# A four-layer graph network on one core: operands of VectorE moved to PSUM, and the last pass's factors moved to ScalarE

## The reference

```python
# layer 0: attention with clipped scores, 8 heads of 16
score = exp(clip(sum(K[src] * Q[dst]) / 4, -5, 5));  out = sum_dst(V[src] * score) / (sum_dst(score) + 1e-6)
# layer 1: edge features through a small network, weights from the degrees
agg = sum_dst((x[src] + relu(edge_attr @ W1e) @ W2e) * w[src] * w[dst])
# layer 2: radial weights of each edge from two silu layers, times scalars and vectors of the source
msg = combine(w_edge, xs[src], xv[src], direction);  out = sum_dst(msg) @ W_out
# layer 3: attention by channel, with a softmax over the edges of a node
e = leaky_relu(feat_src[src] + feat_dst[dst]);  a = exp(e - max_dst(e)) / sum_dst(...);  out = sum_dst(a * v[src])
```

## Time and profile before

| | before |
|---|---|
| median of 3 runs | 5067.57 us (5067.40 to 5072.91) |
| the profiled execution | 5068.24 us, its span 5066.5 us |
| PE, DVE, ACT, POOL busy | 3567.9, 3633.2, 2770.5, 3623.2 us |

### The profile page before, as it was taken

How to read it: one execution, slowest core, us unless ns; L and a number is a source line. 1 busy time by engine, 2 the same in 40 slices (tenths; PEclk the granted TensorE clock), 3 DMA queues, 4 the chain that set the end, 5 groups by cost and what they waited for, 6 DMA issues and landing times. The chain is left out here.

```text
span 5066.5 us, 96049 instructions
## 1 busy us (share of the span) xinstructions
PE 3567.9 (70%) x20064; PEld 2948.3 (58%) x20065; DVE 3633.2 (72%) x8844; ACT 2770.5 (55%) x6960; POOL 3623.2 (72%) x3861
## 2 busy tenths in 40 slices
PE   5444444453376666666778888888879999999993
PEld 4444444443265555555556666666657777777772
DVE  5666666666654444444677777777759999999998
ACT  2444444444632222222467666666648888888885
POOL 3777777775677777777367777777727877777773
PEclk7777777776687777777879999999889999999996
DMA  6444444443333333333121121122137777777772
GB/s 184 156 154 155 154 153 150 152 154 99 114 87 77 79 78 78 78 78 79 33 63 56 56 56 56 56 56 57 52 98 194 194 195 196 195 196 196 196 195 56
DMA packets 491118, 596.80 MB, mean 118 GB/s; under 512 B 127483, under 2 KB 349165, under 8 KB 490639
## 3 DMA queue, kind: packets, MB, share of 16 engines
q0 software_dynamic: 141696, 349.47, 25.5%
q1 hardware_dynamic: 348463, 245.90, 16.3%
q10 hardware_dynamic: 864, 0.39, 0.0%
HBM read 505.89 MB, written 30.07 MB: 106 GB/s over the span
## 5 line engine op out<-in xcount | busy, mean ns | idle before, releaser
L916 DVE TENSOR_TENSOR acc<-acc,banks 128x256 f32 (+1 forms) x3520 | 1339.5, 381 | 625.2 <-PE banks L892 432.4
L831 POOL DMA_INDIRECT e_rows<-kv_t,e_index x820 | 805.6, 982 | 249.8 <-issue 245.5
L892 PE MATMUL banks<-e_rows,e_sel 128*128 128x256 f32 x3520 | 971.0, 412 | 13.4 <-ACT e_sel L875 8.4
L831 POOL DMA_INDIRECT e_rows<-x_t,e_index x820 | 795.9, 971 | 257.0 <-issue 243.8
L831 POOL DMA_INDIRECT e_rows<-up_t,e_index x820 | 775.2, 945 | 249.9 <-issue 206.6
L831 POOL DMA_INDIRECT e_rows<-fsv_t,e_index x820 | 784.7, 957 | 219.9 <-issue 219.9
L867 ACT ACTIVATE e_away<-node_iota,local 128x128 f32<-128x128 f32 x2640 | 840.6, 390 | 8.1
L892 PE MATMUL banks<-e_msg,e_sel 128*128 128x137 f32 (+1 forms) x3520 | 753.7, 363 | 8.9 <-DVE acc L916 4.6
L892 PEld LDWEIGHTS banks<-e_rows,e_sel 128*128 128x128 f32 x3520 | 667.1, 205 | 146.9 <-DVE acc L916 48.7
L993 PE MATMUL banks<-acc,e_sel_t 128*128 x1760 | 312.4, 333 | 581.5 <-DVE e_sel_t L960 567.0
L1118 ACT ACTIVATE e_rows<-banks,e_rows 128x128 f32<-128x128 f32 x880 | 251.4, 370 | 795.2 <-PE banks L1109 404.2
(11 more groups left out here) (207 smaller groups left out, 6388.6 us busy)
## 6 DMA issues: line engine op xcount, KB each, us to landing
e_near<-near_d SPq DMA_DIRECT2D x440, 258.0 KB, 5.3
e_far<-acc SPq DMA_DIRECT2D x880, 64.0 KB
e_attr<-in_attr_rows SPq DMA_DIRECT2D x880, 32.0 KB
e_rows<-kv_t,e_index POOLq DMA_INDIRECT x820
e_rows<-x_t,e_index POOLq DMA_INDIRECT x820
e_rows<-up_t,e_index POOLq DMA_INDIRECT x820, 2.4
e_rows<-fsv_t,e_index POOLq DMA_INDIRECT x820
kv_t<-proj_kv SPq DMA_DIRECT2D x12, 512.0 KB
```

What stands on the lines that cost most here:

```text
L831: G.indirect_dma_start(out=self.rows[:, u, i, 0:self.width], out_offset=None, in_=self.table, in_offset=bass.IndirectOffsetOnAxis(ap=index ...
L892: m = PE.matmul(bank[n_bank][:, col + at:col + at + rows.shape[1]], self.place_of_sel(g)[:, i, :], rows, start=True, stop=True)
L916: V.tensor_tensor(to, to, bank[n_bank][:, col:col + self.sums].unsqueeze(1), ALU.add).then_inc(self.s_added[i], 1)
```

## The change

In pass 1 ACT takes the exponential of the scores twice: into `msg` as before, and a second time into a PSUM bank of its own (6 or 7 by turns), where `message` now reads them. In pass 2 the row of node numbers is copied once to PSUM bank 7, and `select` reads it there. In pass 4 `shrinks` and DVE's `at_firsts` go. DVE computes the fall of the maximum, one number per channel (`drops`); ACT computes the distance of every node number to the group's first node, times 2^14 (`from_first`), and then exp(fall minus distance), which is the factor at the first node and zero elsewhere (`at_firsts`). The values' product is split by channels: GpSimd takes channels 0 to 15 of all four items, DVE channels 16 to 127. The stages of pass 4 are in another order, and `first_row` shares memory with `top`.

```diff
@@ -845,12 +846,12 @@
 
             engine.wait_ge(self.s_sums[-1], g.upto(k))
 
-        def select(self, g):
+        def select(self, g, iota):
 
             if g.old(self.sels):
                 self.summed(V, g, -self.sels)
             V.tensor_tensor(self.place_of_sel(g),
-                            node_iota[:].unsqueeze(1).to_broadcast([P, GROUP, P]),
+                            iota.unsqueeze(1).to_broadcast([P, GROUP, P]),
                             local[:, ds(g.n * GROUP, GROUP)].unsqueeze(2).to_broadcast([P, GROUP, P]),
                             ALU.is_equal).then_inc(self.s_sel, 1)
...
@@ -968,7 +969,7 @@
     def edges0():
         with Phase(nc, "e0") as ctx:
             ps = EdgePass(ctx, kv_t, 2 * D, W0)
-            B_Q = (4, 5)
+            B_Q, B_S = (4, 5), (6, 7)
...
@@ -1019,14 +1020,21 @@
                 A.wait_ge(s_clip, g.upto(0))
                 if g.old(SPAN):
                     ps.summed(A, g, -SPAN)
-                A.activation(msg[:, g.at(SPAN), :, D:D + HEADS0], clip[:, g.r2, :].rearrange("p (i h) -> p i h", i=GROUP),
-                             ACT.Exp, scale=0.25).then_inc(s_score, 1)
+                of = clip[:, g.r2, :].rearrange("p (i h) -> p i h", i=GROUP)
+                A.activation(msg[:, g.at(SPAN), :, D:D + HEADS0], of, ACT.Exp, scale=0.25)
+                if g.old(2):
+                    A.wait_ge(s_msg, g.upto(-2))
+                A.activation(scores(g), of, ACT.Exp, scale=0.25).then_inc(s_score, 1)
+
+            def scores(g):
+
+                return bank[B_S[g.r2]][:, 0:GROUP * HEADS0].rearrange("p (i h) -> p i h", i=GROUP)
 
             def message(g):
                 V.wait_ge(s_score, g.upto(0))
                 V.tensor_tensor(msg[:, g.at(SPAN), :, 0:D].rearrange("p i (h c) -> p i h c", c=HDIM0),
                                 ps.row(g)[:, :, D:2 * D].rearrange("p i (h c) -> p i h c", c=HDIM0),
-                                msg[:, g.at(SPAN), :, D:D + HEADS0].unsqueeze(3).to_broadcast([P, GROUP, HEADS0, HDIM0]),
+                                scores(g).unsqueeze(3).to_broadcast([P, GROUP, HEADS0, HDIM0]),
                                 ALU.mult).then_inc(s_msg, 1)
...
@@ -1085,9 +1093,14 @@
             attr = ps.sb("attr", [ED + 1, SPAN, GROUP, P])
             s_attr = [ps.sem(f"attr{u}") for u in range(SPAN)]
             s_h, s_relu, ones = ps.sem("h"), ps.sem("relu"), ps.sem("ones")
-            B_H = (4, 5)
+            B_H, B_IOTA = (4, 5), 7
             V.memset(attr[ED:ED + 1, :, :, :], 1.0).then_inc(ones, 1)
             PE.wait_ge(ones, 1)
+            V.tensor_copy(bank[B_IOTA][:, 0:P], node_iota[:]).then_inc(ones, 1)
+            V.wait_ge(ones, 2)
+
+            def select(g):
+                ps.select(g, bank[B_IOTA][:, 0:P])
...
@@ -1190,7 +1203,7 @@
                     A.activation(side(own), x[:, own, :], ACT.Copy, scale=eps1[:]).then_inc(s_own, 1)
 
             ps.run([(0, gather), (1, hidden), (3, sums), (2, weighted), (4, ps.add(0)), (4, ps.add(1)),
-                    (4, ps.add(2)), (4, ps.add(3)), (0, ps.select), (0, radial), (0, own_parts)],
+                    (4, ps.add(2)), (4, ps.add(3)), (0, select), (0, radial), (0, own_parts)],
                    [(d_emb.sem, ITEM_TILES * 32), (d_rhat.sem, ITEM_TILES * 16), (s_own, N_BLOCKS)])
...
-            rise, shrink = ps.sb("rise", [P, 1]), ps.sb("shrink", [P, 2])
+            drop, gap = ps.sb("drop", [P, 2]), ps.sb("gap", [P, 2, P])
...
-            first_row = ps.sb("first_row", [1, N_GROUPS])
+            first_row = top[0:1, 0, 0:N_GROUPS]
...
             V.wait_ge(spread_heads, 1)
-            V.tensor_scalar(firsts[:], bank[B_F][:, 0:N_GROUPS], 1.0 / STEP, None, ALU.mult).then_inc(start, 1)
+            V.tensor_scalar(firsts[:], bank[B_F][:, 0:N_GROUPS], APART / STEP, None, ALU.mult).then_inc(start, 1)
             V.tensor_scalar(others[:], bank[B_F][:, 0:N_GROUPS], node_step[:], None, ALU.not_equal).then_inc(start, 1)
-            V.wait_ge(start, 7)
-            PE.wait_ge(start, 7)
+            for e in (V, A, PE):
+                e.wait_ge(start, 7)
...
-                    V.wait_ge(s_rise, g.upto(1 - SPAN))
+                    V.wait_ge(s_drop, g.upto(1 - SPAN))
...
-            def shrinks(g):
-
-                A.wait_ge(s_top, g.upto(0))
-                if g.old(1):
-                    A.wait_ge(s_shrink, g.upto(-1))
-                A.activation(rise[:], top_before(g), ACT.Relu, bias=top[:, g.at(SPAN), 0:1], scale=-1.0).then_inc(s_rise, 1)
-                A.wait_ge(s_rise, g.upto(0))
+            def drops(g):
+
+                V.wait_ge(s_top, g.upto(0))
+                if g.old(2):
+                    V.wait_ge(s_first, g.upto(-2))
+                V.tensor_scalar(drop[:, g.r2:g.r2 + 1], top_before(g), top[:, g.at(SPAN), 0:1], 0.0,
+                                ALU.subtract, ALU.min).then_inc(s_drop, 1)
+
+            def from_first(g):
+
+
                 if g.old(2):
                     A.wait_ge(s_first, g.upto(-2))
-                A.activation(shrink[:, g.r2:g.r2 + 1], rise[:], ACT.Exp, scale=-1.0).then_inc(s_shrink, 1)
+                A.activation(gap[:, g.r2, :], node_iota[:], ACT.Abs, bias=firsts[:, ds(g.n, 1)], scale=-APART
+                             ).then_inc(s_gap, 1)
 
             def at_firsts(g):
 
-
-                V.wait_ge(s_shrink, g.upto(0))
+                A.wait_ge(s_gap, g.upto(0))
+                A.wait_ge(s_drop, g.upto(0))
                 if g.old(2):
-                    V.wait_ge(s_f, g.upto(-2))
-                V.tensor_scalar(at_first[:, g.r2, :], node_iota[:], firsts[:, ds(g.n, 1)], shrink[:, g.r2:g.r2 + 1],
-                                ALU.is_equal, ALU.mult).then_inc(s_first, 1)
+                    A.wait_ge(s_f, g.upto(-2))
+                A.activation(at_first[:, g.r2, :], gap[:, g.r2, :], ACT.Exp, bias=drop[:, g.r2:g.r2 + 1], scale=-1.0
+                             ).then_inc(s_first, 1)
...
-            def message(engine, s_msg, items):
+            def message(engine, s_msg, lo, hi):
                 def stage(g):
                     engine.wait_ge(s_exp, g.upto(0))
-                    values = ps.row(g)[:, items, D:2 * D]
-                    engine.tensor_tensor(values, values, ps.row(g)[:, items, 0:D], ALU.mult).then_inc(s_msg, 1)
+                    values = ps.row(g)[:, :, D + lo:D + hi]
+                    engine.tensor_tensor(values, values, ps.row(g)[:, :, lo:hi], ALU.mult).then_inc(s_msg, 1)
                 return stage
...
-            ps.run([(0, gather), (0, load_far), (1, load_resets), (5, message(G, s_msg_g, slice(0, 1))),
-                    (4, below_top), (1, both_ends), (5, factors), (5, sums_a), (2, spread_resets), (5, sums_b),
-                    (5, distance), (2, take), (4, shrinks), (0, turn), (5, at_zero), (4, exps),
-                    (6, scaled), (5, at_firsts), (6, ps.add(0, s_scaled)), (5, message(V, s_msg_v, slice(1, 4))),
-                    (6, ps.add(1)), (3, forward), (6, ps.add(2)), (3, backward), (6, ps.add(3)), (2, leaky)])
+            ps.run([(0, gather), (0, load_far), (1, load_resets), (5, message(G, s_msg_g, 0, 16)),
+                    (4, below_top), (1, both_ends), (5, sums_a), (5, factors), (2, spread_resets), (5, sums_b),
+                    (5, distance), (2, take), (5, at_zero), (4, exps), (5, at_firsts), (4, from_first), (0, turn),
+                    (6, scaled), (5, message(V, s_msg_v, 16, D)), (6, ps.add(0, s_scaled)), (3, forward),
+                    (6, ps.add(1)), (3, backward), (6, ps.add(2)), (2, leaky), (6, ps.add(3)), (4, drops)])
```

9 lines of the change are left out of this document (5 added, 4 removed).

## The result

| | before | after |
|---|---|---|
| median of 14 runs each, in turns | 5068.41 us (5063.48 to 5086.61) | 5059.60 us (5057.23 to 5063.04) |
| profiled execution, its span | 5068.24, 5066.5 us | 5061.25, 5059.5 us |
| first to last gather of pass 1 | 1130.4 | 1113.8 |
| of pass 2 | 1128.8 | 1108.1 |
| of pass 3 | 1100.7 | 1100.1 |

The ratio is 0.9972 (95% interval 0.9962 to 0.9983): 0.3% faster, 9 us, where 69 us were forecast. The last four lines are the starts of each pass's first and last gather in the two traces. Pass 1 gave 16.6 us and pass 2 20.7, and pass 4 took 30.8 back. With 0.6 us of pass 3 that makes 7.1 of the 7.0 us between the spans.

A forecast was written before the change was run, and what follows sets the result against it. The prediction took GpSimd's gathers to bound passes 1 to 3 and DVE to pace pass 4. Its terms, -28 - 21 - 20 = -69 us from 5068.2, gave 4999 us, with a range of 4984 to 5030 us.

The forecast's parts named there:

- What bounds each pass: Whole kernel: GpSimd, with gathers and issue gaps, fills passes 1 to 3; DVE paces pass 4 at 5.38 us a step.
- Pass 2, -21 us: Pass 2: `select` reading node numbers from PSUM shortens gathers from 971 to 945 ns, -21 us (from -23 to -15).
- Pass 1, -28 us: Pass 1: `message` reading scores from PSUM shortens gathers from 982 towards 945 ns, -28 us (between -30 and -16).
- some 10 to 20 hits more, that is 2 to 4 us: Pass 1: more gathers starting inside the SBUF-to-SBUF comparison L960, at 0.19 us a hit, taken off the 30.3 us gain.
- rival of L960 taking over: Pass 1: this comparison meets a gather in each of 220 groups, costing 42 us; 5041 us in all, chance 0.04.
- Products on DVE don't hold up gathers: Passes 1 and 2: something else lengthens gathers, so both passes keep their time; 5048 us in all, chance 0.03.
- Pass 4, -20 us: Pass 4: DVE's step gets 0.09 us shorter over 220 steps, -20 us (from -29 to 0).
- I take 0.09, as `scaled` now stands close behind the sum it waits for: Pass 4, DVE: the step's summed change of -0.10 us was taken as a gain of 0.09 for this closeness.
- L1501's -0.25: Pass 4, DVE: removing this instruction saves 0.25 us a step, its 0.33 us less 0.08 of overlap.
- `drops`, costed at 0.08: Pass 4, DVE: the new one-column instruction adds 0.08 us a step net of overlap, perhaps 0.15.
- TensorE's clock: Pass 4: the granted clock falls from 0.99 to pass 2's 0.78, +255 us, some 5270 us in all; chance 0.03.
- Pass 4 gives nothing: Pass 4: overlapping products or DVE and PE waiting for each other cancel its gain; 5019 us in all, chance 0.13.

## Why the prediction was wrong

- **What bounds each pass** held. GpSimd fills passes 1 and 2, and each nanosecond of a gather is one of the pass. DVE sets pass 4's pace, as the exchange of two of its operations and the shorter DVE product both moved the time by about what they moved on DVE.
- **Pass 2, -21 us** was right: 20.7 us, gathers of 945 ns. The second exponential and the copy to PSUM cost nothing that shows.
- **Pass 1, -28 us** had the right mechanism and a mis-sized term. "some 10 to 20 hits more, that is 2 to 4 us" on L960: there were 57 more (70 for 13), 10 us by themselves, and 820 x (963 - 945) ns = 15 us stayed in all; the run with `turn` on ACT gave it back. The rival of L960 taking over had described it, at the full 42 us and chance 0.04.
- **Products on DVE don't hold up gathers** is refuted: with one operand of one operation in PSUM, and the same gathers, pass 2's took 26 ns less in the mean and pass 1's single ones 0.95 us for 1.29. DVE's own duration stayed (L1027 686 ns, L1035 681). By the Trainium skill's inference (SBUF — State Buffer, Who interferes with whom) both passes would have kept their time; where page and measurement differ here, the measurement decides. The gathers of this kernel also read their indices from SBUF (`e_index` in their rows); whether it is this read that waits, no run tests.
- **Pass 4, -20 us** came out as +31. The step that failed is "I take 0.09, as `scaled` now stands close behind the sum it waits for". It saw the place and gave it 0.01 us. It costs 0.34 us a step. With L1501's -0.25 and the product's +0.06 (its start to the next is 0.53 us for 0.47; 0.07 was foreseen) that makes +0.15 by these terms, and +0.14 by the typical step (5.52 for 5.39), each start being rounded to 0.01. `drops`, costed at 0.08, is hidden in the wait and costs nothing. The late `scaled` at the loop's end, which the prediction had not at all, adds 0.05, so the mean step is 0.19 us longer: 219 x 0.19 = 41 us. That only 31 showed is partly chance: the kernel before lost some 8 us more in its first 45 steps, where products overlapped and single steps took up to 7.0 us, than the changed one did.
- **The cover that was taken away** was not named: the prediction costed the removed, added and resized instructions, and read the new order of the list mainly for what TensorE waits for. That part was right in kind (the wait moved to the sums, 0.48 us a step in place of 0.32), and it was off the path.
- **TensorE's clock** stayed at 0.99. **Pass 4 gives nothing** assumed overlapping products; in after GpSimd's product took 332 ns at 4000 to 4800 us, and 2.07 ns a column was a fair price.
- The chance of a slower pass 4 within a faster kernel had no case of its own. The range ended at 5030 because no rival put a cost on the wait that the change did move.

## What to carry to other kernels

On an engine that runs in order, list the pairs where one operation waits for the one before it, and what stands between them, before a short operation is removed or moved: a separator that pays for a wait is free, and its removal wins next to nothing if the pair is left bare, while taking away a long one cost 0.3 us a step here, of which the idle columns showed little. A loop's branch and the loading of addresses are hidden by the same long operations, so look at the mean step over whole turns of the loop as well as at one step. Where GpSimd makes descriptors for gathers all the time, give DVE's large operations an operand in PSUM, or put them on ACT; both won here. When a change has independent halves, run them apart first: here one gained 40 us and hid that the other lost 30.
